# Order of stores, map waits and accumulating loads on GpSimd's queue in a sign-convolution kernel

## The reference

```
x + (conv(sign(xn), w) + b) * beta_map
```

## Time and profile before

| | us |
|---|---|
| median of three runs | 914.0 |
| lowest and highest | 913.61, 914.13 |
| the profiled execution's own time | 913.99 |
| its span in the profile | 912.2 |
| TensorE busy in the span | 781.0 |
| VectorE busy | 767.2 |
| ScalarE busy | 647.1 |
| GpSimd busy | 139.5 |

### The profile page before, as it was taken

The page is one execution under the profiler, slowest core; times in us unless marked ns, Lnnn a source line. Parts: engine busy times, 40 slices in busy tenths (PEclk is TensorE's granted clock), DMA queues, the critical chain, the costliest instruction groups (busy, mean ns, idle before and its releaser), DMA issues. The chain is left out here.

```text
span 912.2 us, 12812 instructions
## 1 busy us (share of the span) xinstructions
PE 781.0 (86%) x4722; PEld 468.7 (51%) x4722; DVE 767.2 (84%) x1198; ACT 647.1 (71%) x516; POOL 139.5 (15%) x158
## 2 busy tenths in 40 slices
PE   2100019999999999999999999999999999999996
PEld 2100015555656565656565565656565656565654
DVE  4899689999797988888888889797979797979757
ACT  2365648889696978777777777788878696969411
POOL 0089400011011111111111101111111110101011
PEclk9655559999999999999999999999999999999999
DMA  9999962399897888788788889796959596967578
GB/s 381 428 429 428 427 275 80 131 260 274 240 275 221 252 250 243 227 253 229 242 242 234 260 202 299 175 326 156 321 151 314 176 301 193 288 176 212 143 215 246
DMA packets 44874, 232.06 MB, mean 254 GB/s; under 512 B 10928, under 2 KB 11952, under 8 KB 40752
## 3 DMA queue, kind: packets, MB, share of 16 engines
q0 software_dynamic: 17856, 99.56, 42.0%
q1 hardware_dynamic: 26800, 132.05, 38.5%
q10 hardware_dynamic: 192, 0.12, 0.1%
HBM read 179.92 MB, written 51.79 MB: 254 GB/s over the span
## 5 line engine op out<-in xcount | busy, mean ns | idle before, releaser
L705 PE MATMUL acc<-V,U 128*128 128x385 f16 (+1 forms) x4608 | 760.8, 328 | 1.3 <-DVE y L1115 0.8
L705 PEld LDWEIGHTS acc<-V,U 128*128 128x128 f16 x4608 | 451.4, 98 | 306.4 <-DVE y L1115 1.4
L548 ACT ACTIVATE sn<-acc,inv_s 128x784 f32<-128x784 f32 x126 | 114.4, 908 | 162.5 <-PE acc L705 158.3
L388 POOL DMA_DIRECT2D y<-x x62 | 53.3, 860 | 703.6 <-DVE y L1126 690.5
L507 ACT ACTIVATE T<-low 128x2352 f16<-128x2352 f32 x60 | 127.3, 2122 | 0.9 <-DVE D L1047 0.9
L1126 DVE SCALAR_TENSOR_TENSOR y<-y,cst,bmap 128x1568 f32<-128x1568 f32 x63 | 115.7, 1836 | 0.1
L522 ACT ACTIVATE r<-xb,ab 128x1568 f32<-128x1568 f32 x64 | 106.7, 1690 | 5.5 <-ACT low L497 4.0
L497 ACT ACTIVATE low<-xb,ab 128x1624 f32<-128x1624 f32 x60 | 102.2, 1703 | 0.2
L511 ACT ACTIVATE T<-T 128x1568 f16<-128x1568 f16 x58 | 87.6, 1510 | 1.9
L665 PE MATMUL low<-mv,cst 128*128 128x32 f32 x2 | 0.6, 397 | 85.0 <-DVE mv L825 85.0
L1047 DVE TENSOR_TENSOR D<-T 128x1568 f16<-128x1568 f16 x60 | 58.4, 972 | 13.8 <-ACT T L511 13.8
(11 more groups left out here) (163 smaller groups left out, 517.4 us busy)
## 6 DMA issues: line engine op xcount, KB each, us to landing
xb<-x SPq DMA_DIRECT2D x60, 812.0 KB, 6.4
y<-x POOLq DMA_DIRECT2D x62, 784.0 KB, 8.4
out<-y POOLq DMA_DIRECT2D x62, 784.0 KB, 9.3
bmap<-map_rows SPq DMA_DIRECT2D x32, 784.0 KB, 7.1
xb<-x SPq DMA_DIRECT2D x10, 1568.0 KB, 18.6
y<-x SPq DMA_DIRECT2D x10, 1568.0 KB, 18.2
r<-x SPq DMA_DIRECT2D x5, 1568.0 KB, 18.0
sn<-x SPq DMA_DIRECT2D x5, 1568.0 KB, 18.8
```

Of the source, the lines that this page charges most:

```text
L388: pool.dma_start(y[:, g], x_v[n, g % 2, g // 2], accum_op=ALU.add).then_inc(x_added[g], 16)
L548: nc.scalar.activation(kept, sums, ACT.Copy, scale=inv_s[:, b:b + 1]).then_inc((snap1, snap2)[half], 1)
L705: return nc.tensor.matmul(into, U[:, ci, digits, k, dx, co * P:(co + 1) * P], plane, start=(planes is FIRST and i == 0), stop=(planes is T ...
```

## The change

In GpSimd's loop the call that stores the previous group moves from behind the next group's addition of x to ahead of the wait for the next group's `scaled`. In the old order GpSimd waits for `scaled` of group s, issues addition s, waits for the landing of addition s - 1, issues store s - 1. In the new order it waits for the landing of addition s - 1, issues store s - 1, waits for `scaled` of group s, issues addition s. Nothing else is changed; the number and the sizes of the transfers are the same.

```diff
             for s in range(G4 * NI - 2):
                 n, g = divmod(s, G4)
+                if s:
+                    store(s - 1)
                 pool.wait_ge(scaled, s + 1)
                 pool.dma_start(y[:, g], x_v[n, g % 2, g // 2], accum_op=ALU.add).then_inc(x_added[g], 16)
-                if s:
-                    store(s - 1)
             store(G4 * NI - 3)
```

## The result

The changed kernel took 917.6 us in the median of six runs (916.28 to 919.12), the kernel before 914.03 us in six (913.61 to 914.75). The ratio is 1.0037 with a 95% interval of 1.0027 to 1.0048, which is 3.4 us (2.5 to 4.4) slower. The changed kernel's runs spread over 2.8 us, those of the old one over 1.1 us. In a longer series the old kernel's spread is 2.3 us (913.53 to 915.85, 34 runs; one more, at 939.4 us and a lower granted clock, is left out). The profiled execution took 916.28 us, and it is the fastest of the six, so its trace shows less than the whole loss.

What follows compares the result with a forecast made beforehand. TensorE was taken as the bound, at four groups of 11.88 us per image. Slots 0, additions 0, round trip 0 and end +1.0 on the profiled 913.99 gave 915.0 us, range 913.5 to 917.5.

Steps and rivals of the forecast that it cites:

- Stores, earlier: GpSimd's stores in the loop go out earlier and free slots of `y`; gain 0, bounds 0 and -0.8 us.
- Additions, later: In the loop each addition waits for the previous one's landing, up to 2 us late but covered; cost 0, bounds 0 and +1.
- The two queues: SP's channel-sum round trip beside GpSimd's transfers: small store ends some 2 us earlier, load takes 2 to 4 us; value 0.
- the load is caught: Rival, chance 0.09: the moved store holds the channel-sum load at `crow`, images 2 to 14; TensorE stands 3.3 us each, 957 us.
- the prediction's limit: Channel-sum load at `crow`: TensorE is delayed only where the load takes over 5.1 us from its issue at 435.8.
- The rival's slack: Channel sums: 1.2 us left between the end of `ends(n, 0)` at 449.1 and TensorE's need at 450.3.
- The end: Last groups: addition 61 goes behind store 60, store 61 leaves at 906.6 and lands at 912.1; cost +1.0, bounds 0 and +2.5.
- The end slips further: Rival, chance 0.20: displaced transfers at the end cost their full 3.1 us each, store 61 lands at 916.3; 916.6 us.
- Nothing shows: Rival, chance 0.10: at the end only the 2.0 us count, store 61 lands at 910.1, still hidden; 914.0 us.
- faster: Rival, chance 0.04: slot waits or TensorE's 0.8 us count after all, or VectorE's end is relieved; 912.0 us at best.

Runs made afterwards that it cites:

- last two groups alone: Kernel before, with the new order only for groups 60 and 61: 915.9 us, ratio 1.0021.
- old end: Changed kernel, but with the old order for the last three groups (59, 60, 61): 915.3 us, ratio 1.0017.
- new start alone: Kernel before, with the new order only for groups 0 to 16: 916.1 us, ratio 1.0028.
- 42 groups of the new order in the middle: Changed kernel, but with the old order for groups 0 to 16 and the last three: 913.8 us, ratio 0.9998.
- the collision made on purpose: Kernel before, but the addition of group 1 in images 1 to 14 also waits until `cs98` is written: 929.5 us, ratio 1.0165.
- the guard: Changed kernel with last three groups in old order; group 1's addition in images 1 to 14 waits for the next image's channel sums to load: 913.8 us, 0.9996.
- that of 919.75 us: Profiled execution of the changed kernel with GpSimd itself adding x to group 61 by an instruction, not a DMA; that kernel measured 918.3 us, 1.0047.

## Why the prediction was right, and where it was not

The time lies at the upper edge of the range of 913.5 to 917.5: 917.6 us by the median, 917.4 by the ratio. The direction had a chance of only 0.29; the largest, 0.67, was on a time within 0.2%. The forecast was +1.0 us; +3.4 was measured, made of two parts. The end is 1.9 us (last two groups alone; 1.8 by the difference of 1.0037 and 1.0017). The start is 1.6 us (old end, 0.4 to 2.7) or 2.6 us (new start alone, 1.6 to 3.7). That the range holds the result is in part luck: its upper side was there for a slipping end, and nearly half of the loss came from the additions, for which the sum had 0.

*Stores, earlier: 0.* Right. TensorE ran on with and without the slot waits, and 42 groups of the new order in the middle cost and gain nothing (0.9998).

*Additions, later: 0, bounds 0 and +1.* This step failed. I took the landing times of the old order for the new one (a median of 8.4 us, the slowest 2 us over the interval), and the lateness as a single slip of up to 2 us. In the first 17 groups of the changed kernel additions land after 8.4 to 16.1 us, 10.8 in the mean, where the old order had 6.7 to 11.9 and 8.8. Each waits for the one before, so the lateness adds up, to 10.2 us at group 8. It also goes away slowly. In images 1 to 3 of the changed kernel the four landing times of an image add up to 44 us, and with the issues between them the chain needs about 47 us for an image of 47.5. From image 5 on, with the additions on time, the four take 32 to 35 us. Why a late addition lands later was not tested.

I also named the wrong things behind the late addition. The slot held, but not by my sum: from `finish` to the overwriting it is mostly 27 to 32 us and not 23.8, a store now lands sooner, and in the tightest place 2.3 us were left (store 6 landed at 278.3, `mid` at 280.6). What suffers is a transfer in the other queue that the addition now meets.

*The two queues: 0.* The first half held. SP's wait for the small store is 2.3 us shorter in the mean (75.0 less 38.5 over 16), and in the image of the earlier trace rows VectorE had the channel sums at 437.8, 1.9 us earlier. The rival "the load is caught" had the right victim but the wrong culprit and place. It made the moved store the cause, in 13 images. In images 6 to 15 that store goes out 0.1 us behind the load, which takes 1.6 to 1.9 us as before. A store that goes out ahead of the load does hold it, but not for long enough to cost: in image 4 of the changed kernel it went out 0.35 us ahead and landed at 343.1, and VectorE had the sums at 343.3, after 4.25 us, where the prediction's limit is 5.1. The addition that goes out late ahead of the load is the culprit. An edge shows in the traces: with the addition 0.03 to 0.57 us ahead the load took 2.8 to 3.3 us (six images), with 0.64 to 1.8 us ahead 7.3 to 8.2 us, and with 3.25 us ahead 6.0 us.

The rival's slack was right too. From the issue of the small store to VectorE's having the sums 7.27 us pass in the earlier trace rows; with the slack of 1.2 that makes 8.5 us. In all 19 stalls of the traces that show one after 225 us, what this time is over 8.5 us is TensorE's stall, within 0.15 us.

By the Trainium skill's page "DMA: Bandwidth & Descriptors", section "Queues, rings and completion order", a completion lands only after all earlier writes of the same engine, whatever the queue. Five loads that VectorE had within 0.25 us of the addition's landing agree (299.4, 300.0, 441.6, 583.8 and 680.5 us), as does that of the earlier trace rows. In the experiment with the collision made on purpose the load came 2 us behind the addition and ahead of the store, which shows that the rule alone does not give the time. Which descriptors hold the load was not tried.

*The end: +1.0.* The mechanism was right, the size was off. Store 61 was to leave at 906.6 and left at 907.3; addition 61 was 3.3 us late where 2 to 3 was said. Mis-sized were two things. Store 61 lands after 4.0 us, not 5.5, so it never became last itself (911.3). And its company stretched the last two parts by 2.1 us, where I had put 0.6.

*The end slips further.* The time lies in this rival's 915.8 to 918.6, but its mechanism did not occur: store 61 was to leave as late as 910.8 and to land last, at 916.3. It left at 907.3 and landed ahead of the two parts.

*Nothing shows, and faster:* excluded. 2.5 us is the lower bound of the loss.

A version that beats the kernel before was not found. New order with all additions of group 1 guarded and the old end gives 913.8 us, 0.9996 (0.9987 to 1.0005), the same.

## What to carry to other kernels

A wait put ahead of an issue makes everything behind it on that queue a chain. Ask what the chain does where landing times are longest, and not at their median, and whether it is fast enough to catch up: here it needed 47 us of 47.5, and a bad start lasted for up to nine images. A big transfer that slips by a few microseconds can catch a small one in another queue, and the small one may be what the bounding engine has 1 us of slack for. Compare the spread of the runs too: 6.8 against 1.4 us with the new start alone pointed to a collision that its profiled execution, the fastest, did not show. That the slow executions are such collisions is shown by the guard, which took the spread down to 0.9 us; of the slow executions with a new start only that of 919.75 us was profiled.

## What the runs showed of the hardware that I had not expected

A load of 36.8 KB that takes 1.85 us undisturbed took 7.3 to 8.2 us when an addition of 784 KB from the other queue had been issued 0.64 to 1.8 us ahead of it. Stores of 784 KB with no addition of their queue just ahead of them land after 3.6 us at best and 5.1 in the median, where they took 9.3 us as second of a pair. And GpSimd's elementwise addition of two SBUF tiles (3.5 us) stopped VectorE's with two SBUF inputs for its whole length: 5.13 us for an instruction of 1.79. In the old order two instructions of `ends`, which read one input from PSUM, ran beside it in their usual 0.63 and 0.62 us. The Trainium skill, page "SBUF — State Buffer", section "SBUF: two separate sides", describes this as an exclusive lock on a shared port pair, held for the whole instruction; 3.52 and 5.13 us agree with it.
